# A graph convolution whose row gathers are issued two pairs ahead of the last landing in place of three

## The reference

```
x = x + relu_conv2(relu_conv1(layernorm(x)))        # each: segment_max(x[src], dst) @ W_rel.T + b + x @ W_root.T
x = x + ffn(layernorm(x))                            # 8 experts, the 512 best tokens of each, GELU, scatter-add
```

## Time and profile before

| | |
|---|---|
| median of 3 runs | 944.09 us (943.99 to 945.03) |
| profiled execution, span | 1025.1 us |
| PE busy (share of the span) | 726.0 us (71%) |
| DVE busy | 681.6 us (66%) |
| POOL busy | 546.7 us (53%) |
| ACT busy | 270.3 us (26%) |
| gathers L838 | 372 instructions, 389.5 us, from 146.8 to 802.6 us |
| moved on the gather queue's kind (software) | 124.74 MB, 44.6% of 16 engines |

### The profile page before, as it was taken

One profiled execution on the slowest core, in us unless ns is written; L12 is line 12 of the kernel. 1 busy time (PEld: TensorE's weight loads), 2 busy tenths in 40 slices (PEclk: granted clock), 3 DMA queues, 4 the chain that ended last, 5 costly groups with the idle time before them and its releaser, 6 DMA issues.

```text
span 1025.1 us, 9702 instructions
## 1 busy us (share of the span) xinstructions
PE 726.0 (71%) x2541; PEld 329.5 (32%) x2541; DVE 681.6 (66%) x1232; ACT 270.3 (26%) x389; POOL 546.7 (53%) x537
## 2 busy tenths in 40 slices
PE   0317555778378778866488657887698678789996
PEld 0214222333133323322133323333243235344442
DVE  3768565588758767873888774898588879733120
ACT  0264250222022202222434030343243122012222
POOL 5652326557746675764556655566447200565644
PEclk9757877899789989987899878998899889899999
DMA  5715336557746675656657756666566400377656
GB/s 136 219 36 183 101 97 184 162 170 214 216 116 194 184 218 144 202 168 184 174 177 214 226 163 180 189 213 193 158 193 187 143 12 1 113 235 142 105 102 82
DMA packets 64770, 162.18 MB, mean 158 GB/s; under 512 B 16383, under 2 KB 20755, under 8 KB 64709
## 3 DMA queue, kind: packets, MB, share of 16 engines
q0 software_dynamic: 40448, 124.74, 44.6%
q1 hardware_dynamic: 17004, 17.16, 6.0%
q10 hardware_dynamic: 7272, 19.74, 5.9%
HBM read 143.37 MB, written 18.11 MB: 158 GB/s over the span
## 4 chain that ended last, share of the span: by engine, by line
PE 33%; DVE 25%; issue 19%; another core or an unknown queue 9%; ACT 5%; POOL 3%; DMA 2%; DVEq 2%; POOLq 0%; ACTq 0%; SPq 0%
PE pp L1165 8%; DVE acc L891 6%; PE prow L1136 5%; PE pp L1563 5%; DVE weights L902 5%; PE pp L1576 4%; PE prow L1103 3%; PE prow L1124 2%; DVE mem L1403 2%; POOL mem L838 1%; DMA mem<-tab,ic 1%; PE pp L1346 1%; PE prow L519 1%; PE pp L501 1%
## 5 line engine op out<-in xcount | busy, mean ns | idle before, releaser
L838 POOL DMA_INDIRECT mem<-tab,ic x372 | 389.5, 1047 | 266.9 <-issue 136.5
L1165 PE MATMUL pp<-weights,slots 128*128 128x512 bf16 x1200 | 306.8, 405 | 114.8 <-DVE acc L891 70.2
L891 DVE TENSOR_TENSOR acc<-acc,pp 128x1024 f32<-128x1024 f32 x180 | 219.1, 1217 | 85.3 <-PE pp L1165 33.5
L1165 PEld LDWEIGHTS pp<-weights,slots 128*128 128x128 bf16 x1200 | 118.0, 103 | 307.5 <-issue 103.8
L902 DVE TENSOR_TENSOR weights<-weights,mem 128x1024 f32<-128x1024 f32 x129 | 158.1, 1226 | 17.9 <-DVE weights L902 11.3
L1136 PE MATMUL prow<-weights,aggT 128*128 128x512 f32 x160 | 92.2, 708 | 37.4 <-ACT aggT L1213 20.5
L1124 PE MATMUL prow<-weights,rootT 128*128 128x512 f32 x160 | 76.0, 619 | 0.0
L1615 POOL DMA_INDIRECT out<-mem,node_of x28 | 44.2, 1577 | 47.3 <-ACT mem L1593 40.9
L1544 DVE COPY weights<-prow 128x512 f32<-128x512 f32 x28 | 18.7, 688 | 72.1 <-PE prow L1103 71.7
L1604 POOL DMA_INDIRECT mem<-xnd,slot_of x20 | 22.0, 1099 | 78.4 <-DVE weight_of L1538 72.6
L1213 ACT ACTIVATE aggT<-prow 128x512 f32<-128x512 f32 x20 | 11.9, 597 | 192.5 <-PE prow L1103 98.7
(11 more groups left out here) (349 smaller groups left out, 828.0 us busy)
## 6 DMA issues: line engine op xcount, KB each, us to landing
slots<-ttd ACTq DMA_DIRECT2D x20, 640.0 KB
mem<-tab,ic POOLq DMA_INDIRECT x372
weights<-in_L_ffn_W SPq DMA_DIRECT2D x9, 512.0 KB, 5.1
weights<-in_L_ffn_W ACTq DMA_DIRECT2D x7, 512.0 KB
xnd<-xin ACTq DMA_DIRECT2D x10, 256.0 KB
mem<-in_x SPq DMA_DIRECT2D x2, 1120.0 KB
tab<-mem SPq DMA_DIRECT2D x1, 2240.0 KB
weights<-in_L_gnn_W_rel SPq DMA_DIRECT2D x2, 1024.0 KB
```

The source lines that it names most:

```text
L838: g.indirect_dma_start(ring[:, h * PAIR + k, :], None, tables[l], bass.IndirectOffsetOnAxis(ic[:, j * PAIR + k:j * PAIR + k + 1], 0))\
L891: v.tensor_tensor(acc[:, :, :], acc[:, :, :], pp[j % 2][:, :, :], ALU.max).then_inc(S["pa"], 1)
L1165: ins = t.matmul(pp[j % 2][:, i, :], sel[u][:, j * KP + i, :], hot[:, j, w, :], start=w == 0, stop=w == 2)
```

## The change

One constant goes from 3 to 2. The start value of `ready` and the constants in DVE's waits follow it. GpSimd may now issue a pair when the pair two in front of it has landed, in place of three in front.

```
-FLYING = 3
+FLYING = 2
```

## The result

The changed kernel takes 987.81 us (median of 5 runs, 980.47 to 989.46) against 944.09 us (5 runs of before, 938.68 to 945.03): ratio 1.0456, 95% interval 1.0416 to 1.0495. It is 4.6% slower. The forecast was 0.6% slower with a range up to 958 us, so the direction was right and the size was wrong by a factor of eight.

What follows compares the result with a forecast made beforehand. No engine was full; gathers were mostly early, held by the ring's six places, so only late pairs cost. 3.5 + 1.0 + 0.9 = 5.4 us on the 944.09 us median gave 949.5 us, range 944.5 to 958.

Steps and rivals of the forecast that it cites:

- to over 60: GpSimd's idle time before gathers at L838, released by a landing, should rise from 16 us to over 60.
- I put the difference on the median as it is.: The 5.4 us found on the 1025.1 us profile was added to the 944.09 us median, giving 949.5 us.
- hand rules: All 186 pairs retimed by previous gather's end, freed place and landing two in front, each keeping its issue-to-landing time.
- The turn of 5.6 us: Steady gathers: two pairs take 4.8 us to landing plus 0.8 us path, 2.8 us a pair against 2.5.
- 26 us for a tile: Gathers at 2.8 us a pair, 9.3 pairs a tile, need 26 us in place of 23.
- Heavy tile of layer 0, +3.5.: Pairs at 238 to 270 us end up 3.5 us late, and DVE's loop waits for them: +3.5 us.
- First tile of layer 1, +1.0: Third pair, issued during the table load, starts later and DVE waits at L920: +1.0 us (0 to 4.3).
- Heavy tile of layer 1, +0.9: Three pairs issued back to back just ahead of use; the third waits for the first one's landing: +0.9 us.
- L920 elsewhere, 0.: DVE's later reads of the third pair in three other tiles are covered by TensorE's work: 0 (0 to 2.6).
- The gathers become the bound: Rival: every gather delay counts and none is covered, 11.3 us, 955.4 us; chance 0.27.
- Faster: Rival: at layer 1's start the table load gets its turn sooner; 941.5 us at best; chance 0.07.
- Register instructions, 0.: DVE's 19 added register instructions: 1.9 us if bare, 0 where covered; taken as 0.

Runs made afterwards that it cites:

- C4: Chip of the fourth experiment group; the unchanged kernel before took 942.88 us there, ratio 0.9992, with no hold-ups.
- C1 to C3: Chips of the first three experiment groups; the unchanged kernel before took 1022.94, 1044.01 and 1048.24 us there, with hold-ups.
- C1: Chip of the first experiment group; the unchanged kernel before took 1022.94 us there, ratio 0.995 to its other runs.
- x2: Kernel before with DVE's 19 register instructions added and three pairs still allowed in flight: 1035.12 us, ratio 1.0032.
- x8: Kernel before with only one pair allowed in flight (`FLYING = 1`): 1536.83 us, ratio 1.4636.

## Why the prediction was wrong

- **Where the change costs.** The mechanism was right: the wait for landings grows from 16 us "to over 60" (85.6; on C4 it starts from 42.6), the wait for the ring shrinks, pairs in steady stretches stand further apart, the heavy tile of layer 0 is longer. Places and sign held.
- **"I put the difference on the median as it is."** This is the step that failed: 5.4 us, worked out on a profile of the one kind of chip, were put on a time of the other, where the change costs 43.7 us. Applied to the profile of C4, which has no hold-ups, the same hand rules give 46.3 us if everything counts, of which 18.5 us are waits at L920 outside the first tile of layer 1, where TensorE may cover them; so 28 to 46 us. Measured from that profile to the first one of the changed kernel: 978.7 - 943.1 = 35.6 us. (The 43.7 us of the medians are more, as the profiled run of the changed kernel is 7.3 us under its median and that of C4 0.8 us above 944.09.) By this the rules were nearly sound and their input was not. The first profile had 42.7 us of hold-ups, in which gathers went on and DVE did not read, so pairs looked early that are just in time in the timed runs; the first two tiles of layer 0, for one, take 34.8 us each in it and 30.2 and 27.2 on C4. Layer by layer, in busy time per stretch on C4 and in the changed kernel:

```profile
133.70:427.80 294.10, 233.79 (x824) 98.21 (x839) 231.22 (x211) 63.84 (x51) 209.09 (x196) 0.93 0.67 198
427.80:734.10 306.30, 237.12 (x901) 105.24 (x920) 258.48 (x283) 106.67 (x180) 200.11 (x193) 0.92 0.69 205
```
```profile
133.70:447.00 313.30, 234.36 (x839) 97.37 (x836) 231.28 (x211) 63.88 (x51) 211.51 (x197) 0.92 0.64 186
447.00:768.20 321.20, 242.40 (x919) 105.89 (x920) 258.33 (x283) 106.65 (x180) 212.98 (x193) 0.91 0.67 196
```

  The columns are the stretch, its length, the busy time of PE, weight loads, DVE, ACT and POOL, TensorE's granted clock, the DMA share and GB/s. The length grows by 19.2 and 14.9 us, the busy time of DVE not at all, and that of TensorE by 0.6 and 5.3: for DVE it is all waiting.
- **The turn of 5.6 us.** Mis-sized: 5.5 + 0.8 = 6.3 us for two pairs, 3.1 for one (the median distance of the changed kernel's pairs is 3.08) against 2.8. It did not enter the 5.4 us, since the rules let each pair keep its own time; it stands behind the rival's 26 us for a tile.
- **Heavy tile of layer 0, +3.5.** From its first read to that of the next tile it takes 36.4 us on C4 and 44.9 in the changed kernel, +8.5. **First tile of layer 1, +1.0:** 53.5 us from the last tile's first read to its own, against 55.9, and 34.3 against 34.4 inside it; with the end of layer 0 in it, +2.5. **Heavy tile of layer 1, +0.9:** 38.7 and 43.8, +5.1. Of the rest, which I had at 0, most stands in two of the tiles with 11 pairs: k = 6 +5.0, k = 16 +6.1.
- **L920 elsewhere, 0.** DVE's wait there went from 20.0 to 39.4 us (C4 against changed). The 46.3 of the rules were above the 35.6 measured, so some of it is covered, as I said, but not all.
- **The rivals.** "The gathers become the bound" named the 81 us and the right mechanism, with 0.27, and I priced it from the same stretched profile. "Faster" named the wrong mechanism; on C1 to C3 it would have had the sign right by luck. I had no rival in which the hold-ups decide, though the 10.8 us stood in the trace.
- **Register instructions, 0.** Held on C1 (x2, no change that can be told); not run on a chip of the other kind.

## What to carry to other kernels

When the profile's span and the median of the timed runs differ by more than the effect that you forecast, find out first what fills the difference: look for instructions whose releaser ended long before they start, and compare with a profile from another chip. A limit on transfers in flight is priced by the mean time from issue to landing plus the path back to a started issue, divided by the limit, against the rate at which the consumer reads when nothing else holds it up. And a change of a few per cent may have one sign on one chip and the other on the next, so it should be judged on more than one.

## What the hardware did that I had not expected

- The same kernel took 943 us on one chip and 1027 to 1053 us on four others, while two pairs in flight took 988 us in the first comparison and 1009 to 1013 us on three of those four. With the gathers slowed (by the limit or by pacing) the spread is 22 to 25 us in place of 84 to 110, and most of what is left lies outside the gathers.
- At up to 15 hand-overs from TensorE to ScalarE in the layers of a run the copy started 0.5 to 17.1 us late (the longest in x2), and DVE waited up to 4.7 us for its own last instructions ahead of the gathers, with no record of what went on. The granted clock over the span is 0.913 in the profile of before on C4, and 0.873 to 0.895 in those of the same kernel with hold-ups. The clock alone does not make them: four transposes with a modelled 0.66 us were followed by a wait of 10.8.
- A gather that waits for a landing starts 0.8 to 0.9 us after it (484.5 to 485.27 in the earlier trace rows; 708.4 to 709.20 and 702.4 to 703.33 in x8), and this shows only when the wait is really waited for.
